# Two sequences of a context tile multiplied apart, each in half of the array's rows, in the value product of layer 2

## What is computed

```python
qh = (q_in @ wq + bq); kh = (kv_in @ wk + bk); vh = (kv_in @ wv + bv)      # heads of K = 128
kh = jnp.concatenate([kh, bias_k], axis=1); vh = jnp.concatenate([vh, bias_v], axis=1)
logits = jnp.einsum('bqhk,bthk->bhqt', qh, kh) / scale
weights = jax.nn.softmax(logits, axis=-1)
ctx = jnp.einsum('bhqt,bthk->bqhk', weights, vh).reshape(b, q_len, H * K)
return ctx @ wo + bo
```

## Time and profile before

| | us |
|---|---|
| median of three runs | 2194.09 |
| lowest and highest of them | 2193.95, 2196.76 |
| the profiled execution, as timed | 2198.78 |
| its span, first to last instruction | 2197.0 |
| granted clock of TensorE over the span | 0.955 |

### The profile page before, as it was taken

One profiled execution on the slowest core, in us unless ns is written; L12 is line 12 of the kernel. 1 busy time (PEld: TensorE's weight loads), 2 busy tenths in 40 slices (PEclk: granted clock), 3 DMA queues, 4 the chain that ended last, 5 costly groups with the idle time before them and its releaser, 6 DMA issues.

```text
span 2197.0 us, 39924 instructions
## 1 busy us (share of the span) xinstructions
PE 2004.4 (91%) x15392; PEld 1635.2 (74%) x15392; DVE 1183.0 (54%) x2136; ACT 1042.6 (47%) x1935; POOL 1030.4 (47%) x1124
## 2 busy tenths in 40 slices
PE   5887869899999867999999999999999998888698
PEld 3665658844555656989989899898998997866588
DVE  3443544537878855555555455554555545555454
ACT  3543553332323235666565665656566564335532
POOL 5644652126556425545444554545454445146520
PEclk9988988999999789999999999999999999999899
DMA  4010001000000002332323223232232220010000
GB/s 173 2 40 1 1 1 50 1 1 1 1 1 1 29 20 61 90 85 85 93 83 91 85 85 96 83 87 85 85 96 86 85 64 20 20 39 2 1 10 30
DMA packets 61563, 108.10 MB, mean 49 GB/s; under 512 B 6976, under 2 KB 42176, under 8 KB 59968
## 3 DMA queue, kind: packets, MB, share of 16 engines
q1 hardware_dynamic: 60784, 103.34, 15.4%
q10 hardware_dynamic: 592, 2.19, 0.2%
HBM read 103.41 MB, written 2.10 MB: 48 GB/s over the span
## 4 chain that ended last, share of the span: by engine, by line
PE 55%; issue 3%; DVE 3%; POOL 3%; ACT 3%; DVEq 0%; POOLq 0%; ACTq 0%
PE banks L761 17%; PE banks L790 8%; PE banks L833 8%; PE banks L822 5%; PE banks L803 4%; PE banks L577 3%; PE banks L594 3%; PE banks L811 1%; PE banks L426 1%; ACT xn L889 1%; PE banks L403 1%; POOL T L1662 1%; POOL rstd L1637 1%; PE banks L417 1%; DVE bst L1239 1%
## 5 line engine op out<-in xcount | busy, mean ns | idle before, releaser
L1802 POOL TENSOR_TENSOR w_lo<-w2ring,w_hi 128x512 fp32r<-128x512 f32 x128 | 166.4, 1300 | 294.7 <-ACT w_hi L1142 294.7
L1201 ACT ACTIVATE PT<-banks 64x256 f32<-64x256 f32 x256 | 96.7, 378 | 264.6 <-PE banks L811 261.5
L1571 DVE SCALAR_TENSOR_TENSOR c_lo<-banks,cols,c_hi 128x512 fp32r<-128x512 f32 x128 | 96.1, 751 | 223.0 <-ACT c_hi L1166 223.0
L1811 POOL TENSOR_TENSOR wo_lo<-wo_ring,wo_hi 128x256 fp32r<-128x256 f32 x128 | 94.0, 735 | 170.9 <-ACT wo_hi L1172 170.9
L833 PE MATMUL banks<-wo_hi,c_hi 128*128 128x256 f32 x512 | 150.3, 294 | 2.7 <-POOL wo_lo L1811 2.7
L833 PE MATMUL banks<-wo_hi,c_lo 128*128 128x256 f32 x512 | 145.4, 284 | 0.0
L833 PE MATMUL banks<-wo_lo,c_hi 128*128 128x256 f32 x512 | 145.2, 284 | 0.0
L822 PEld LDWEIGHTS banks<-PT,v 128*128 128x128 f32 x1024 | 132.7, 191 | 8.9 <-ACT PT L1201 0.4
L1662 POOL TENSOR_TENSOR T<-T,a_pair 128x1024 f32<-128x1024 f32 x32 | 75.4, 2356 | 130.1 <-DVE T L1313 129.9
L1753 POOL TENSOR_TENSOR rsZ<-stS,r1T 128x512 f32<-128x512 f32 x64 | 97.0, 1521 | 83.4 <-DVE stS L1459 44.8
L822 PE MATMUL banks<-PT,v 128*128 128x128 f32 x1024 | 134.9, 275 | 0.3 <-ACT PT L1201 0.3
(11 more groups left out here) (212 smaller groups left out, 5932.5 us busy)
## 6 DMA issues: line engine op xcount, KB each, us to landing
w2ring<-in_w SPq DMA_DIRECT2D x128, 384.0 KB, 3.0
b2ring<-in_b SPq DMA_DIRECT2D x128, 128.0 KB, 3.4
wo_ring<-in_wo SPq DMA_DIRECT2D x128, 128.0 KB, 2.2
mlp_w<-in_mlp SPq DMA_DIRECT2D x6, 1024.0 KB, 5.7
wl<-in_wres SPq DMA_DIRECT2D x1, 2656.0 KB, 8.9
X<-in_x_in SPq DMA_DIRECT2D x4, 512.0 KB, 11.8
ctx_tok<-in_ctx_in SPq DMA_DIRECT2D x4, 512.0 KB, 15.9
wb<-in_wres SPq DMA_DIRECT2D x2, 1024.0 KB, 12.1
```

The costliest lines, as they stand in the source:

```text
L1201: A(PT2[keys_of, n % 2, :, r, :], held(("tp2", n))[keys_of, 0:2 * P].rearrange("p (i q) -> p i q", i=NT), ACT.Copy)\
L1571: V.scalar_tensor_tensor(c_lo[:, n % CR, :], held(("pv2", n))[:, :], col(biv, n % H2), c_hi[:, n % CR, :].bitcast(f32), ALU.add, ALU.subtr ...
L1802: G.tensor_tensor(w2_lo[:, n % 2, :], w2ring[:, n % 3, 0:2 * KT * P], w2_hi[:, n % 2, :].bitcast(f32), ALU.subtract).then_inc(S["l2_wlo"], 1)
```

## The change

The values of the two sequences of a tile are multiplied in two matmuls. That of sequence r has the 64 keys of r as rows, stands in rows 64r to 64r+63 of the array, has all 128 features as columns, takes 64 query columns, and writes to a PSUM bank of its own. So `PT2` needs no zeros and half of the room, and one ScalarE copy of 128 partitions fills it; `weigh` takes two banks of the ring where it took one, and has eight matmuls of 64 columns where it had four of 128. ScalarE's `c_hi` and VectorE's `c_lo` are written in two instructions of 256 columns, one for each bank, where there was one of 512. The zeroing on GpSimd and ScalarE's wait for it go.

```diff
                     def weigh(n):
-                        pe.wait_ge(S["l2_PT"], 2 * n + 2)
+                        pe.wait_ge(S["l2_PT"], n + 1)
                         pe.wait_ge(S["l2_v"], 2 * (n // 2) + 2)
-                        b = take(pe, ("pv2", n), "l2_c", n + 1)
+                        out = [take(pe, ("pv2", n, r), "l2_c", 2 * n + r + 1) for r in range(2)]
                         for i in range(NT):
                             u, a = divmod(i, 2)
-                            out = b[:, u * 2 * P:(u + 1) * 2 * P].rearrange("p (r a q) -> p a r q", r=2, a=2)[:, a]
-                            last = mm(out, v2[:, n % 2, i, :], PT2[:, n % 2, i].rearrange("p r q -> p (r q)"), start=True, stop=True)
+                            for r in range(2):
+                                keys_of = slice(r * SEQ, (r + 1) * SEQ)
+                                last = mm(out[r][:, i * SEQ:(i + 1) * SEQ], v2[keys_of, n % 2, i, :],
+                                          PT2[keys_of, n % 2, u, a * SEQ:(a + 1) * SEQ], start=True, stop=True, tile_position=(r * SEQ, 0))
                         last.then_inc(S["l2_pv"], 1)
...
-                        A(c_hi[:, n % CR, :], held(("pv2", n))[:, :], ACT.Identity, bias=col(name(n, "biv"), n % H2)).then_inc(S["l2_chi"], 1)
+                        for r in range(2):
+                            A(c_hi[:, n % CR, :].rearrange("p (u r x) -> p r u x", u=2, r=2)[:, r],
+                              held(("pv2", n, r))[:, 0:2 * P].rearrange("p (u x) -> p u x", u=2), ACT.Identity,
+                              bias=col(name(n, "biv"), n % H2)).then_inc(S["l2_chi"], 1)
...
-                        for r in range(2):
-                            keys_of = slice(r * SEQ, (r + 1) * SEQ)
-                            A(PT2[keys_of, n % 2, :, r, :], held(("tp2", n))[keys_of, 0:2 * P].rearrange("p (i q) -> p i q", i=NT), ACT.Copy)\
-                                .then_inc(S["l2_PT"], 1)
+                        A(PT2[:, n % 2].rearrange("p u q -> p (u q)"), held(("tp2", n))[:, 0:2 * P], ACT.Copy).then_inc(S["l2_PT"], 1)
...
-                        dve.wait_ge(S["l2_chi"], n + 1)
-                        V.scalar_tensor_tensor(c_lo[:, n % CR, :], held(("pv2", n))[:, :], col(biv, n % H2), c_hi[:, n % CR, :].bitcast(f32),
-                                               ALU.add, ALU.subtract).then_inc(S["l2_c"], 1)
+                        for r in range(2):
+                            dve.wait_ge(S["l2_chi"], 2 * n + r + 1)
+                            hi, lo = (x[:, n % CR, :].rearrange("p (u r x) -> p r u x", u=2, r=2)[:, r] for x in (c_hi, c_lo))
+                            V.scalar_tensor_tensor(lo, held(("pv2", n, r))[:, 0:2 * P].rearrange("p (u x) -> p u x", u=2), col(biv, n % H2),
+                                                   hi.bitcast(f32), ALU.add, ALU.subtract).then_inc(S["l2_c"], 1)
...
-                    G.memset(PT2, 0.0).then_inc(S["pt_zero"], 1)
```

More of the change, by code:

```diff
@@ L250, in build @@
         v2 = view(at("v2", A + 13328, 2 * TOK), "p (s t d) -> p s t d", s=2, t=NT)
-        PT2 = view(at("PT2", A + 14352, 2 * NT * P), "p (s i r q) -> p s i r q", s=2, i=NT, r=2)
+        PT2 = view(at("PT2", A + 14352, 2 * 2 * P), "p (s u q) -> p s u q", s=2, u=2)
         wv_hi, wv_lo = (view(at(n, M + 2048 + 1024 * i, 2 * KT * 2 * P, f32r), "p (s k h d) -> p s k h d", s=2, k=KT, h=2)
@@ L298, in build @@
         names = """mlp_in mlp_in2 wo_in0 wo_in1 wo_in2 wo_in3 w2_in0 w2_in1 w2_in2 out_done
-            masks_ready slots_zero pt_zero vbd_preset ctx_tp ctxT_ready
+            masks_ready slots_zero vbd_preset ctx_tp ctxT_ready
             dve_step pool_step
@@ L808, in turn @@
                         pe.wait_ge(S["l2_prob"], n + 1)
-                        b = take(pe, ("tp2", n), "l2_PT", 2 * n + 2)
+                        b = take(pe, ("tp2", n), "l2_PT", n + 1)
                         for u in range(2):
@@ L827, in project @@
                         pe.wait_ge(S["l2_wolo"], n + 1)
-                        pe.wait_ge(S["l2_c"], n + 1)
+                        pe.wait_ge(S["l2_c"], 2 * n + 2)
                         for t in range(NT):
@@ L1178, in cross2 @@
                     query(0)
-                    act.wait_ge(S["pt_zero"], 1)
                     for n in range(NH):
```

## The result

The changed kernel takes 2237.44 us (median of four runs, 2233.67 to 2239.86) against 2195.43 for the kernel before (four runs, 2193.95 to 2197.29): the ratio is 1.0189, with a 95% interval of 1.0172 to 1.0207. The forecast was 2236.6. The profiled execution took 2239.86.

A forecast was written before the change was run, and what follows sets the result against it. TensorE's own time was taken to bound layer 2: +0.335 us in each of 128 steps gives +42.9, less 0.4 for ScalarE's last copy, so 2236.6 us on the median of 2194.09; range 2222 to 2258.

The forecast's parts named there:

- TensorE sets the end of layer 2: In layer 2 TensorE is busy 120.00 of 120.00 us, so each us added to it is paid in full.
- weigh before: In each layer 2 step, weigh's eight records at 0.111 us each take 0.89 us in the kernel before.
- pairs go side by side at the load's pace: In weigh, the two row halves load together: 8 pairs at 0.111 us, the same 0.89 us as before.
- streaming fewer columns brings nothing: In weigh, a float32 load of 128 columns costs 0.11 us by itself; streaming fewer columns does not shorten the record.
- a change of shape and back: Around weigh, switching the array to 64 rows and back makes each step 0.335 us longer, 128 times: +42.9 us.
- banks, ScalarE, VectorE: In layer 2, no new bank wait; ScalarE net -0.13 us a step, VectorE +0.22, neither on the path.
- other stages: Outside layer 2, the stages would keep their times to 2 us.
- sum: Whole kernel: 2198.8 + 42.9 - 0.4 = 2241.3 us against its own execution; 2236.6 on the median, +1.9%.
- The price of the edges: At weigh's start and end: going in 0.20 us less 0.015, going out 0.20, taken from L675, L648 and L417.
- rival 1: In weigh, loads of 64 rows cost half, a pair takes 0.058 us: -5 us, 2189 us; chance 5%.
- bounds of +31 to +55 us: Layer 2 cost: low if one end lacks the 0.09 us without a load, high if pairs are paced at 0.125.
- loads take turns: In weigh, the halves' loads alternate, 16 records at 0.111 us: 1.22 a step, +157 us, 2351 us; chance 7%.

The follow-up runs named there:

- two-bank kernel: The kernel before with weigh's result in two banks and the split ScalarE and VectorE evacuations, matmuls unchanged: 2201.29 us, ratio 1.0011.
- in turn: The changed kernel with the four matmuls of the first sequence, then the four of the second, instead of alternating: 2310.53 us, ratio 1.049.
- all rows: The changed kernel with all 128 rows in each of the eight matmuls, sequences not separated, output not the reference's: 2309.6 us, ratio 1.0475.
- visits: Two runs against the changed kernel: weigh cut into two visits a step, 2286.74 us; two heads' weigh in one visit every second step, 2228.66 us.
- four-quarter kernel: The changed kernel with each of the eight matmuls cut into two of 64 features, array tiles 64 by 64: 2194.41 us, ratio 0.9974.

## Why the prediction was right, point by point

The kernel took 2237.4 us where 2236.6 was forecast: +42.0 against +42.5 over each one's own median of before. That the two times agree to 0.8 us is in part luck, since the four runs of the changed kernel span 6.2 us; the agreement of the steps is not. The prediction's own steps, against what was measured:

| step of the prediction | forecast | measured | shown by |
|---|---|---|---|
| TensorE sets the end of layer 2 | no wait for the others | busy 1005.3 of 1006.0 us | windows, chain |
| weigh before | 8 x 0.111 | 0.89 | and the two-bank kernel |
| pairs go side by side at the load's pace | 0.111 apart, ~10 ns within | 0.111, 6 to 7 ns | load starts; in turn costs +0.50 |
| streaming fewer columns brings nothing | - | full-row records with 64 streamed columns: 0.112 each | all rows |
| a change of shape and back | 0.335 a step | +0.33; 0.33 saved with one fewer, 0.38 paid for one more | chain, visits |
| banks, ScalarE, VectorE | nothing | loop 964.4, as before | two-bank kernel |
| other stages | within 2 us | before and after the change: 851.6 and 851.7 ahead of the loop, 380.5 and 380.2 behind it | start and end of the loop |
| sum | +42.9 - 0.4 | +41.3 in the loop, +42.0 in the median | times |

So the deciding step held: L633's loads with 16 streamed columns had shown that a float32 record of 128 weight columns is bound by its load, and the four-quarter kernel turned this into a test, since there only the load's columns were halved (each record still streams 64), and the pace fell from 0.111 to 0.058. The price of the edges, taken from other shapes in other stages, was right to 0.01 us a step (41.3 us in 127 steps are 0.325); that the idle time ahead, 0.35, is the same for 64 by 64 was not known then. The Trainium skill (TensorEngine Tiling (Array Packing), Tiling Modes) says that a change of the tiling mode drains TensorE and gives no figure for it; the trace agrees, with 0.35 us in which no load runs ahead of the visit, and 0.33 us a visit here. The "up to 2x" of its Overview, rival 1, is seen against the same sixteen records with all rows (0.111 us a pair, 0.112 a record), and not against the kernel before, which needs only eight. Rival 1's 0.058 a pair is that of the scores' unrounded starts; from its rounded row it would be 0.063, at which the change is worth nothing either way.

Two sizes were off, both off the path. ScalarE was to have 0.13 us a step less and has 30.1 less in the loop (580.11 - 550.00), 0.24 a step. The copy into `PT2` saves 0.37 a step, as forecast; the slip is in `c_hi`, which costs 0.15 more and not 0.24, since two halves in a row take 0.84 together and not two times 0.463: the second begins before the first has ended. VectorE was to have 0.22 more and has 3.8 us more in the loop (499.77 - 495.99), 0.03 a step. There too the two halves of `c_lo` overlap: in the loop its group grew from 94.6 to 110.3 us of busy time, 0.12 a step. The rest is the product at the end of the softmax (`P`), which the change does not touch and which went from 93.5 to 81.7. I had summed durations of single instructions that overlap; on the engine that sets the end, 0.1 us a step of such a slip would be 13 us.

The bounds of +31 to +55 us were wider than the cost turned out to need, and the 7% for "loads take turns" was a real risk: the order in turn, which differs from the change in the nesting of two loops, costs 0.50 us a step, 64 us over the changed kernel.

What stays open is the time behind the loop. It is 380.2 to 380.5 us in the kernel before, the changed one, those with two banks, with all rows and with two visits; and 385 to 391 us in the others, where the code there is the same but the granted clock is lower. A shorter loop is not what they share, since the two sequences in turn, with a loop 64 us longer than the changed kernel's, have 390.5. Nor does it take a changed loop to lower the clock: of 23 executions of the kernel before that ran beside four of these, seven have a granted clock of 0.950 to 0.952 over the span and take 2201.9 to 2204.9 us, the other 16 have 0.955 to 0.957 and take 2194.5 to 2200.3. All twelve of the quarters have 0.948 to 0.951. With one trace for each kernel it is not shown that the longer time belongs to the kernel and not to the execution, and a gain of 1% or less among the times above can hold some of it. What makes TensorE spend more time at the 1.2 GHz level there was not found, and no run was made for it.

## What to carry to other kernels

Before splitting a matmul into row halves, find out what paces its records: take the pace of a matmul with the same weight columns and few streamed ones. If the two are alike, the load sets it, two half-row matmuls side by side take as long as a whole one, and only fewer weight columns are faster (64 by 64 quarters went at 0.058 us against 0.111). Count each change of the array's shape as a fixed price, 0.33 us here, and gather what has the same shape into few visits, next to work that changes the shape anyway; alternate the halves record by record.

And when the engine that sets the end gets shorter, look again at who was hidden behind it: here shorter steps of TensorE called up waits for other engines (GpSimd's key bias, then VectorE's softmax), and moving two small tasks by a step gave most of that back.

## What the runs showed of the chip that I had not expected

- TensorE behaves as if it looked only some four records ahead for one that can run in the free half of the array: eight records of one half and then eight of the other take 11.5 record times from the first start to the last, where alternating ones take 7. The Trainium skill (TensorE: Matmul & The Clock Gate, Part 2) speaks of a reorder window that is 64 deep for loads, by which the second half's loads could have started with the first; here the ninth record did not start before 0.50 us (1262.090 - 1261.589), and the measurement decides.
- Four quarters of the array load and multiply within 20 ns of each other (starts at 1261.815, .821, .828 and .835) and go at 0.058 us a four.
- A visit added to a step costs 0.37 to 0.39, one taken away gives 0.33.
- Unchanged code behind the loop took 380 us in five kernels and 385 to 391 us in seven, with 39 us at the 1.2 GHz level in the first kind and 48 to 72 in the second, in one traced execution of each.
